# One decay factor made ahead of an activation table visit, and the output products moved behind it, in a fused selective-scan and mixture-of-experts layer

## The reference

```
u, res = split(x @ W_in);  u = silu(conv3(u));  dt, Bm, Cm = split(u @ W_x)
delta   = softplus(dt @ W_dt + b_dt);  A = -exp(A_log)
deltaA  = exp(delta * A);  deltaB_u = delta * u * Bm
h_t = deltaA_t * h_(t-1) + deltaB_u_t;   y_t = sum_n h_t * Cm_t
out = (y + u * D) * silu(res) @ W_out;   x1 = layernorm(x + out)
```

## Time and profile before

| | |
|---|---|
| median of 3 runs | 2871.32 us (2870.43 to 2873.97) |
| profiled execution, its time | 2872.2 us |
| its span in the profile | 2870.4 us |
| granted TensorE clock, mean of the span | 0.943 |
| DVE busy | 2202.7 us (77%) |
| PE busy | 2393.8 us (83%) |
| ACT busy | 1796.2 us (63%) |
| scans run from | 88.1 us to about 1803.5 us |
| start of the scans of chunks 6 and 7 | 734.87 and 843.15 us |

### The profile page before, as it was taken

The page is one execution under the profiler, slowest core; times in us unless marked ns, Lnnn a source line. Parts: engine busy times, 40 slices in busy tenths (PEclk is TensorE's granted clock), DMA queues, the critical chain, the costliest instruction groups (busy, mean ns, idle before and its releaser), DMA issues. The chain is left out here.

```text
span 2870.4 us, 48365 instructions
## 1 busy us (share of the span) xinstructions
PE 2393.8 (83%) x15726; PEld 1889.4 (66%) x15726; DVE 2202.7 (77%) x3230; ACT 1796.2 (63%) x3358; POOL 1793.9 (62%) x837
## 2 busy tenths in 40 slices
PE   7799989989989989989999976426888898898891
PEld 2466666666666666666666665326888888888891
DVE  0698888888898888888898899567567567567554
ACT  3688878778788788778788886202334334334334
POOL 0787887887787887887888887111443443433424
PEclk9999999999999999999999989657999999999996
DMA  2112112112112111121111121102132132122116
GB/s 65 52 38 67 60 53 67 60 53 67 52 61 67 49 64 61 51 67 51 63 60 59 52 67 52 59 0 67 31 78 56 31 77 58 31 74 60 31 16 242
DMA packets 84421, 170.11 MB, mean 59 GB/s; under 512 B 8480, under 2 KB 52000, under 8 KB 84144
## 3 DMA queue, kind: packets, MB, share of 16 engines
q1 hardware_dynamic: 68784, 145.72, 14.9%
q0 software_dynamic: 15360, 20.98, 4.6%
HBM read 130.49 MB, written 36.18 MB: 58 GB/s over the span
## 5 line engine op out<-in xcount | busy, mean ns | idle before, releaser
L347 POOL TENSOR_TENSOR dbu<-du,b_all 128x2048 f32<-128x2048 f32 x256 | 1161.2, 4542 | 168.5 <-DVE hst L532 168.5
L426 ACT ACTIVATE da<-delta,a_neg 128x512 f32<-128x512 f32 x1024 | 706.0, 691 | 258.8 <-DVE hst L532 252.7
L532 DVE TENSOR_TENSOR_SCAN hst<-da,dbu 128x512 f32<-128x512 f32 x512 | 601.2, 1210 | 133.0 <-ACT da L426 130.6
L532 DVE TENSOR_TENSOR_SCAN hst<-da,carry,dbu 128x512 f32<-128x512 f32 x512 | 631.3, 1269 | 53.8 <-ACT da L426 51.8
L617 PEld LDWEIGHTS w<-ident,hst 128*128 128x128 f32 x2048 | 233.2, 142 | 416.8 <-ACT hTC L414 270.8
L1367 PE MATMUL gu<-x_part,w_part 128*128 128x256 f32 x3840 | 483.1, 285 | 24.3 <-DVE silu L1207 15.4
L1367 PEld LDWEIGHTS gu<-x_part,w_part 128*128 128x128 f32 x3840 | 468.3, 193 | 28.9 <-DVE silu L1207 18.4
L617 PE MATMUL w<-ident,hst 128*128 128x128 f32 x2048 | 325.4, 282 | 193.0 <-ACT hTC L414 166.4
L510 DVE SCALAR_TENSOR_TENSOR yacc<-hd,c_tok,yacc 128x512 f32<-128x512 f32 x512 | 376.2, 735 | 69.5 <-PE hd L617 67.8
L1114 POOL DMA_INDIRECT acc_dram<-eo,token x80 | 129.4, 1617 | 458.2 <-ACT eo L1309 432.2
L555 PE MATMUL gen<-xT,w_u 128*128 128x512 f32 x768 | 395.0, 605 | 14.4 <-DVE w_u L495 12.9
(11 more groups left out here) (183 smaller groups left out, 2851.5 us busy)
## 6 DMA issues: line engine op xcount, KB each, us to landing
b_all<-b_rows SPq DMA_DIRECT2D x128, 512.0 KB, 3.7
xT<-in_xT SPq DMA_DIRECT2D x16, 514.0 KB, 5.1
x_rows<-in_x SPq DMA_DIRECT2D x16, 512.0 KB, 4.9
x_dram<-x SPq DMA_DIRECT2D x16, 512.0 KB, 3.1
acc_dram<-x SPq DMA_DIRECT2D x16, 512.0 KB, 5.3
w_raw<-in_wg SPq DMA_DIRECT2D x8, 1024.0 KB
w_raw<-in_wu SPq DMA_DIRECT2D x8, 1024.0 KB
w_raw<-in_wd SPq DMA_DIRECT2D x8, 1024.0 KB
```

The source lines that it names most:

```text
L347: nc.gpsimd.tensor_tensor(dbu[DBU[n]][:], du[parity][:], b_n, ALU.mult).then_inc(dbu_ready, 1)
L426: nc.scalar.activation(da_bank[t % 2][:], delta[parity][:, t, :], ACT.Exp, scale=a_neg[:, t, n:n + 1]).then_inc(da_ready, 1)
L532: nc.vector.tensor_tensor_scan(hst[DBU[n]][:, t, :], da_bank[t % 2][:], dbu[DBU[n]][:, t, :], initial, ALU.mult, ALU.add).then_inc(scanned, 1)
```

## The change

At slot 20 ACT makes two factors: that of slot 20 in its own bank, and that of slot 21 in `gen_bank[1]`. The scan of slot 21 reads it there. The table visit moves from slot 19 to behind them in slot 20. So that the ring's bank 1 is free, `o0` and `o1` move from slots 14 to 20 to slots 22 to 25, and `o1` waits for the scan of slot 21. Nearly all that follows moves by one or two slots.

```
-           "o0": (0, 14, 15, 16, 17, 18), "o1": (1, 20, 20, 20, 20, 20), "xd": (0, 22, 23, 24, 25),
-           "u0": (1, 24, 25, 26, 27, 29, 30), "cT": (0, 28), "d0": (0, 31), "d1": (1, 33), "d2": (0, 35),
+           "o0": (0, 22, 22, 22, 22, 22), "o1": (1, 23, 23, 24, 24, 25), "xd": (0, 24, 25, 26, 27),
+           "u0": (1, 28, 29, 30, 31, 32, 33), "cT": (0, 30), "d0": (0, 33), "d1": (1, 35), "d2": (0, 37),
...
-BEFORE_TURN = ("o1",)
+BEFORE_TURN = ("o0",)
+BORROW_AT = 21
...
-SILU_AT, STATS_AT, EXP_AT, LN_AT, NORM_AT = 19, (22, 24), (41, 42), (43, 44), (45, 46, 48, 49)
+SILU_AT, STATS_AT, EXP_AT, LN_AT, NORM_AT = 20, (25, 27), (43, 44), (45, 46), (47, 48, 49, 50)
...
-                    if s.main:
+                    if s.main and slot != BORROW_AT:
...
+                    if s.main and slot == BORROW_AT - 1:
+
+                        nc.scalar.activation(gen_bank[1][:], delta[parity][:, t + 1, :], ACT.Exp,
+                                             scale=a_neg[:, t + 1, n:n + 1]).then_inc(da_ready, 1)
...
+                        da = gen_bank[1] if slot == BORROW_AT else da_bank[t % 2]
...
+                        if name == "o1" and s.main:
+                            pe.wait_ge(scanned, c * 64 + BORROW_AT + 1)
```

More of the change, by code:

```diff
@@ L41 @@
 FILL_AT = {"r0": (0, 0, 1), "r1": (1, 2, 3), "C0": (0, 4), "C1": (1, 6), "r2": (0, 9, 10), "r3": (1, 11, 12),
[4 rows of a table removed]
-READ_AT = {"r0": 4, "r1": 6, "C0": 7, "C1": 9, "r2": 13, "r3": 15, "o0": 21, "o1": 23, "xd": 27, "cT": 30, "u0": 32,
-           "d0": 33, "d1": 35, "d2": 38, "d3": 40, "u1": 47, "ud0": 50, "u2": 53, "xt0": 53, "xt1": 56, "ud1": 59,
-           "u3": 61, "lg": 62}
-BEFORE_TURN = ("o1",)
[4 rows of a table added]
+READ_AT = {"r0": 4, "r1": 6, "C0": 7, "C1": 9, "r2": 13, "r3": 15, "o0": 23, "o1": 26, "xd": 29, "cT": 32, "u0": 34,
+           "d0": 35, "d1": 37, "d2": 40, "d3": 42, "u1": 49, "ud0": 52, "u2": 54, "xt0": 54, "xt1": 57, "ud1": 59,
+           "u3": 62, "lg": 62}
+BEFORE_TURN = ("o0",)
+BORROW_AT = 21
 O_BLOCKS = ((2, 3), (0, 1))
@@ L531, in chunk @@
                         initial = carry[:, n, t:t + 1] if parity == 1 else 0.0
-                        nc.vector.tensor_tensor_scan(hst[DBU[n]][:, t, :], da_bank[t % 2][:], dbu[DBU[n]][:, t, :],
+                        da = gen_bank[1] if slot == BORROW_AT else da_bank[t % 2]
+                        nc.vector.tensor_tensor_scan(hst[DBU[n]][:, t, :], da[:], dbu[DBU[n]][:, t, :],
                                                      initial, ALU.mult, ALU.add).then_inc(scanned, 1)
```

## The result

The changed kernel takes 2935.16 us (median of 4 runs, 2932.36 to 2937.72) against 2870.88 for the kernel before (4 runs, 2867.54 to 2873.97): ratio 1.0222, interval 1.0210 to 1.0234. **The change costs 64 us.** The forecast was 2919, range 2894 to 2938.

A forecast was written before the change was run, and what follows sets the result against it. DVE's single line of scans and additions bounds a balanced kernel, with PE's list deciding behind the visit. 3.5 us a chunk, 45 for thirteen, plus 2 and 1 for chunks 14 and 15, on 2871.3: 2919, range 2894 to 2938.

The forecast's parts named there:

- The sign: Whole kernel: the change makes it slower, given a chance of 0.89.
- the mechanism: Behind the visit: o moved there lengthens PE's list, hd turns come late, and DVE cannot give the lag back.
- The visit: Slots 20 to 22: DVE's stall of about 4.2 us moves to before scan 22; gain 0.1 us a chunk.
- The chain on PE: Slots 22 to 27: hd turns of slots 25 and 27 start at +6.35 and +10.8 us; slot 27's addition 0.8 late.
- Rival C: Behind the visit: PE is not the bound, one more scan is covered, 18 us faster, 2853 us; chance 0.06.
- `cT`, the read of `u0`: Slots 28 to 36: shared cT slot and later read make slot 31's addition 1.9 us late, slot 35's 3.0 (odd).
- Slot 47: Late slots: u1 and u2 both have a part in slot 47; 0.7 us more a chunk, waits in 49 and 51.
- The end slots: Around slot 60: xt1 behind the turn, lg beside a u3 part; one wait shrinks about 0.7, the next grows; minus 0.1.
- the clock: Wherever the scans run: taken to be at its upper level, 2.4 GHz, 9 tenths or more.

The follow-up runs named there:

- borrow_only: Kernel before with only slot 20's factor made in slot 19, in lent bank 1, and o1 waiting for scan 20: 2837.88 us against 2825.88, ratio 1.0041.
- o_behind: Kernel before with o0 and o1 moved behind the visit, to slots 20 to 23, without the borrow: 2879.28 us, ratio 1.0188.
- o_early: Changed kernel with o0 back in slots 14 to 17 and o1 as a lump in slot 22, borrow kept: 2843.99 us, ratio 1.0061.
- ct_alone: Changed kernel with slot 30 left to cT alone, u0 in slots 28 to 34 without 30, read in 36: 2885.29 us in one run.
- u1_single: Changed kernel with u1 one slot earlier, in slots 41 to 46, so slot 47 has one part: 2874.78 us in one run.
- lg61_after: Changed kernel with the router products lg made in slot 61 instead of 60: 2882.97 us, ratio to the kernel before 1.0213.
- lg61_before: Kernel before with the router products lg made in slot 61 instead of 60: 2823.03 us, ratio 0.9997.
- no_borrow: Changed kernel without the borrow, o1's wait on scan 21 kept: 2905.21 us, ratio 1.0280 to the kernel before.

## Why the prediction came out as it did

The sign, the mechanism and the range held, the range with 3 us to spare. The size fell short: chunks 1 to 13 were put at 45 us and took 57, the other three at 3 and took 8. Of the 12 us missing in the thirteen chunks, about 8 arise behind slot 48 (1.35 us in an odd and 1.11 in an even chunk, where 0.6 were forecast) and about 4 at the start of odd chunks, where the clock had fallen (0.54 at slot 18). All that was forecast between slots 18 and 48 came out within 0.2 us a chunk.

**The visit: right.** The stall of 4.18 before scan 22 matches the forecast of about 4.2. In the even chunks, which start with the clock up, scan 22 starts 0.24 earlier than before, against 0.1. `borrow_only` shows the same by itself in the eight chunks without a fall of the clock.

**The chain on PE: right.** It gave +6.35 and +10.8 for the turns of slots 25 and 27 and the rows have 6.35 and 10.80. `o_behind` and `o_early` show that this list, not the borrow, is what costs: with `o` ahead of the visit 45 of the 64 us are gone. How DVE's idle time falls on the slots was not as said: forecast were 1.3 to 2 us at each of the additions of slots 25 and 27, and they are 2.27 and 0.41, with 0.73 before scan 27 for the late factor. The forecast had left out ACT's read of `o1`; it did not change the sum.

**Rival C and the share of weight loads.** PE's weight loads are busy for 69 and 70 of 113 us in the two chunks and 65% of the span. Rival C was to decide if less than 10.0 us passed from the turn of slot 22 to that of slot 27; 10.80 did. The Trainium skill, "Perfetto Trace Analysis", section "Identifying the Most-Contended Engine", would judge TensorE's headroom by MFU and the share of weight loads; read as the prediction reads it, by that share alone, there was room on TensorE and the moved products would have cost nothing. The trace disagrees: DVE waited 2.27 us for a turn behind a row of starts without a gap. The measurement decides: in these ten slots the starts from one to the next tell the headroom.

**`cT`, the read of `u0`: right.** Slots 28 to 36 add 1.94 (odd) and 2.21 (even); forecast 2.2 in an odd chunk (3.0 - 0.8). (The last part of `u0` ends 4.98 us behind the turn of slot 31, about the 5.0 of the forecast; the terms written there add up to 4.86.) `ct_alone`, one run, shows that the `cT` part is real, and that it can't be had back by moving `u0` on.

**Slot 47: nearly right.** 0.7 was taken, 0.57 and 0.51 measured, and `u1_single` gives 0.43 back. The wait was foreseen in slots 49 and 51 both; it stands in slot 51, and slot 49 waits less than before.

**The end slots: the step that failed.** "One wait shrinks by about 0.7, the next grows by as much; minus 0.1" was measured as +0.78 (odd) and +0.60 (even). In an odd chunk before, the additions of slots 59 and 61 wait 0.72 and 0.88; after, the first is nearly gone, as forecast, and the second waits 1.81. PE's turns of slots 59, 60 and 61 show by how much the working had undersized the second. Before, in chunk 7:

```profile
942.70 0.60 PE L617 MATMUL hd<-ident,hst 128*128 128x128 f32 x4
...
944.43 0.60 PE L617 MATMUL w<-ident,hst 128*128 128x128 f32 x4
...
946.58 0.64 PE L617 MATMUL hd<-ident,hst 128*128 128x128 f32 x4
```

And now:

```profile
976.98 0.60 PE L625 MATMUL hd<-ident,hst 128*128 128x128 f32 x4
...
979.02 0.66 PE L625 MATMUL w<-ident,hst 128*128 128x128 f32 x4
...
982.08 0.64 PE L625 MATMUL hd<-ident,hst 128*128 128x128 f32 x4
```

From slot 59 to slot 61 pass 5.10 us, 3.88 before (the means over odd and over even chunks are the same within 0.01). Of these 1.22, 0.91 lie behind the turn of slot 60, where PE now makes a part of `u3` besides `lg`: this part alone is more than the forecast had given to the whole wait. The other 0.31 lie ahead of that turn, and ACT shows why:

```profile
977.18 0.60 ACT L383 ACTIVATE yacc<-gen 128x512 f32<-128x512 f32 x1 [1.91 <-PE gen L580]
```

`ud1` is made in slot 58, no longer 57, and still read in slot 59. ACT stands 1.91 us at that read, 1.34 before; it now starts the read 0.2 us behind PE's turn of slot 59, where it was 1.1 ahead of it. What is behind it in its list comes late: the scale that lets PE's turn of slot 60 go. The working had weighed PE's rows and left out ACT's read, whose distance to its product had shrunk from two slots to one. It had seen just that for `u0`. The rows show the two terms; no run takes either away by itself, and `lg61_after` shows that moving `lg` alone does not win the time back.

**Not foreseen: the clock.** The forecast took the clock to be up wherever the scans run; the earlier trace rows show tenths of a slice of 70 us, too coarse for this. At the start of chunk 7 of the changed kernel PE has stood 3.42 us (2.87 before), and by the clock record the level falls 0.2 us after its work begins: PE's first row, the window, and DVE's waits:

```profile
873.14 0.96 PE L625 MATMUL w<-ident,hst 128*128 128x128 f32 x4 [3.42 <-ACT hTC L415]
```

```profile
872.90:877.90 5.00, 4.76 (x16) 3.10 (x17) 3.57 (x4) 2.29 (x4) 5.00 (x3) 0.66 0.28 88
```

```profile
872.95 2.46 DVE L538 TENSOR_TENSOR_SCAN hst<-da,carry,dbu 128x512 f32<-128x512 f32 x2 [1.49 <-ACT da L427]
876.79 0.75 DVE L515 SCALAR_TENSOR_TENSOR yacc<-hd,c_tok,yacc 128x512 f32<-128x512 f32 x1 [1.38 <-PE hd L625]
```

The turn takes 0.96 where it takes 0.66, and the addition of slot 1 waits 1.38 where it did not wait at all. Chunk 7 is the plainest case and not the typical one, for the kernel before has such falls too. DVE at the start of its chunk 9, behind a stand of PE of 3.30 us:

```profile
1063.25 0.75 DVE L510 SCALAR_TENSOR_TENSOR yacc<-hd,c_tok,yacc 128x512 f32<-128x512 f32 x1 [1.40 <-PE hd L617]
```

Before, chunks 3, 5, 9 and 11 start so, and after, these and chunk 7. At slot 2 the odd chunks lag 0.45 on average (chunk 7 1.48, chunks 5 and 11 0.79 and 0.70, the others 0.15 or less) and the even ones not at all: most of the 0.65 by which the odd ones lag more at slot 22. In chunk 0 the addition of slot 7 waits 1.10 in such a stretch and the scans are 2.0 us late at slot 18, ahead of all that was changed; in chunk 15 a wait of 3.31 behind the `o0` lump follows a fall in slot 21. Over all scans the clock records have the lower level for 78.5 us, 37.5 before. That time is no measure of the loss: in chunks 2, 4, 5, 8, 10 and 11 of the changed kernel the level falls in slot 20 or 21, while `o0` is made in the stall, and these chunks lose as much from scan 18 to scan 28 (0.75 even, 0.87 odd) as those in which it stays up. The Trainium skill, "TensorE: Matmul & The Clock Gate", section "HAM oscillation", describes a matmul kernel in which each wait of TensorE for a transfer makes the work behind it begin cold. The rows here agree in part: behind the stands of 3.12 to 3.48 us at the chunk starts of these two traces the level was down at once or within 1 us, but behind one of 3.78 us it stayed up (`lg61_before`, chunk 5), and in the experiments it fell behind much shorter ones too.

**Open.** What makes the clock fall in one chunk and not in its twin isn't shown by any run, and how much of the 64 us it makes up is known only for the starts of the odd chunks, about 4 us. The changed kernel wasn't run on the chips of the experiments; its place there goes by ratio. The two terms of the end slots (`u3`'s part in slot 60, `ud1` a slot farther from its read) weren't tried alone.

## What to carry to other kernels

Before moving work behind a stall, list what each engine has to do between the end of the stall and the next result that another engine waits for, and add it up from one start to the next: the same rows that are free inside a stall are on the path behind it. When a table of slots is shifted, go through each pair of making and reading and see whether its distance has shrunk; here five shrank to one slot (`o0`, `o1`, `u0`, `xt0`, `ud1`). The read of `u0` goes with some 0.75 us a chunk (slots 34 to 36), that of `ud1` with 0.3; at the read of `o1` ACT stood 2.85 us, which PE's list hid. When a lump is moved into a stretch, look too at what has left that stretch: two terms can hide each other. An engine that gets done early in one place may only wait longer in the next, and for PE that wait can cost clock.

## What was not expected of the hardware

After stands of 1.89 us in even and 2.22 us in odd chunks (`borrow_only`), and of 2.3 to 2.4 us (`no_borrow`), PE's granted clock fell to 1.2 GHz in 5 of 13 and 10 of 13 chunks and stayed at 2.4 GHz in the others. Chunks with the same stand are found in both groups; after one of 3.78 us (`lg61_before`) it stayed up. By the clock record it fell 0.7 to 1.7 us after the work had begun again, and not with its first row. In these two experiments each such fall cost 1.25 to 1.7 us a chunk, as much as a scan; in the stall of the changed kernel it cost nothing.
